# Row fetches for twenty sparse gathers on SP, and five rounds of last layers inside the last tile

## What is computed

```python
seq_embed = jnp.concatenate([emb_seq[i][seq_inputs[:, :, i]] for i in range(NB)], axis=-1)   # 2048 x 40 x 128
item_embed = jnp.concatenate([emb_seq[i][item_inputs[:, i]] for i in range(NB)], axis=-1)    # 2048 x 128
other_info = jnp.concatenate([dense_inputs] + [emb_sparse[i][sparse_inputs[:, i]] for i in range(NS)], axis=-1)
info = jnp.concatenate([q, seq_embed, q - seq_embed, q * seq_embed], axis=-1)
h = jax.nn.sigmoid(info @ att_W1 + att_b1)
h = jax.nn.sigmoid(h @ att_W2 + att_b2)
att = jax.nn.softmax(jnp.where(mask, (h @ att_Wf + att_bf)[..., 0], NEG_INF), axis=-1)
user_info = jnp.einsum('bl,bld->bd', att, seq_embed)
info_all = jnp.concatenate([user_info, item_embed, other_info], axis=-1)      # batch-normalised, then
y = sigmoid(prelu(prelu(info_all @ ffn_W1 + ffn_b1) @ ffn_W2 + ffn_b2) @ out_W + out_b)
```

## Time and profile before

| | us |
|---|---|
| median of 3 runs | 1611.01 (1609.24 to 1612.11) |
| the profiled execution | 1607.81 |
| its span | 1606.0 |
| POOL busy | 1198.4, 75% of the span, 1259 instructions |
| PE busy | 1407.4, 88% |
| DVE busy | 849.7, 53% |
| ACT busy | 398.4, 25% |
| chain that ended last | POOL 72%, issue 24%, PE 3%, DVE 1% |

### The profile page before, as it was taken

How to read it: one execution, slowest core, us unless ns; L and a number is a source line. 1 busy time by engine, 2 the same in 40 slices (tenths; PEclk the granted TensorE clock), 3 DMA queues, 4 the chain that set the end, 5 groups by cost and what they waited for, 6 DMA issues and landing times.

```text
span 1606.0 us, 25922 instructions
## 1 busy us (share of the span) xinstructions
PE 1407.4 (88%) x7602; PEld 776.3 (48%) x7602; DVE 849.7 (53%) x2102; ACT 398.4 (25%) x725; POOL 1198.4 (75%) x1259
## 2 busy tenths in 40 slices
PE   0599999998989988898988888998889998989878
PEld 0355555554545444454544455545455554545432
DVE  5744647463554646365464634646464464636453
ACT  3422213221222212121131222212222221212123
POOL 7877777777777777777777777777777777777773
PEclk9999999999999999999999999999999999999975
DMA  8411121211111121111111112121111112111121
GB/s 165 105 28 47 27 47 28 47 28 27 48 27 48 28 46 29 27 47 28 48 28 47 28 27 48 28 47 28 46 29 27 48 28 46 28 27 28 28 27 14
DMA packets 61501, 63.51 MB, mean 40 GB/s; under 512 B 35845, under 2 KB 36179, under 8 KB 61359
## 3 DMA queue, kind: packets, MB, share of 16 engines
q0 software_dynamic: 40128, 41.17, 12.6%
q1 hardware_dynamic: 19170, 12.53, 3.1%
q10 hardware_dynamic: 2062, 8.08, 1.8%
HBM read 61.57 MB, written 0.11 MB: 38 GB/s over the span
## 4 chain that ended last, share of the span: by engine, by line
POOL 72%; issue 24%; PE 3%; DVE 1%; ACT 1%; POOLq 0%; DMA 0%; DVEq 0%
POOL hist L346 70%; POOL items L346 2%; DVE sums L892 1%; PE pre L530 0%; PE pre L542 0%; PE pre L531 0%; ACT pool L632 0%; PE turned L523 0%; PE pre L442 0%; PE mid L458 0%; PE turned L524 0%; PE pre L444 0%; PE mid L451 0%; DMA hist<-in_L_rec_emb_seq_dram,idx 0%; PE sums L399 0%
## 5 line engine op out<-in xcount | busy, mean ns | idle before, releaser
L346 POOL DMA_INDIRECT hist<-in_L_rec_emb_seq_dram,idx x1184 | 1131.4, 956 | 361.0 <-issue 361.0
L412 PE MATMUL grown<-pool,split 128*128 128x384 bf16 x4704 | 849.6, 330 | 39.7 <-DVE pool L795 39.6
L412 PEld LDWEIGHTS grown<-pool,split 128*128 128x128 bf16 x4704 | 454.5, 99 | 443.9 <-issue 155.5
L795 DVE TENSOR_SCALAR pool<-rel 128x768 bf16<-128x768 bf16 x784 | 382.2, 541 | 0.0
L919 DVE TENSOR_TENSOR prod_t<-turned,item_t 128x512 f32<-128x512 f32 x160 | 109.7, 688 | 401.0 <-ACT hist_t L657 400.8
L662 ACT ACTIVATE hidden<-pre 80x512 f32<-80x512 f32 x160 | 94.9, 593 | 612.7 <-DVE pre L927 601.3
L927 DVE TENSOR_TENSOR pre<-pre,item_part 80x512 f32<-80x512 f32 x160 | 111.0, 694 | 167.5 <-PE pre L444 167.5
L425 PE MATMUL turned<-ident,hist 128*128 128x128 f32 x592 | 99.1, 288 | 86.4 <-DMA hist<-in_L_rec_emb_seq_dram,idx 85.7
L442 PE MATMUL pre<-hist_t,w_hist 128*80 128x512 f32 x320 | 164.4, 595 | 0.0
L444 PE MATMUL pre<-prod_t,w_raw 128*80 128x512 f32 x320 | 163.4, 592 | 0.0
L892 DVE SCALAR_TENSOR_TENSOR sums<-hist,weight,sums 128x128 f32<-128x128 f32 x608 | 159.8, 348 | 0.0
(11 more groups left out here) (110 smaller groups left out, 466.8 us busy)
## 6 DMA issues: line engine op xcount, KB each, us to landing
sparse_rows<-in_L_rec_emb_sparse_dram SPq DMA_DIRECT2D x1280, 0.2 KB
hist<-in_L_rec_emb_seq_dram,idx POOLq DMA_INDIRECT x1184, 2.4
keys<-key_rows SPq DMA_DIRECT2D x28, 384.0 KB
hist<-in_L_rec_emb_seq_dram ACTq DMA_DIRECT2D x6, 672.0 KB
keys<-key_rows ACTq DMA_DIRECT2D x4, 384.0 KB
hist<-in_L_rec_emb_seq_dram ACTq DMA_DIRECT2D x2, 728.0 KB
sparse_rows<-in_L_rec_emb_sparse_dram,idx_sparse POOLq DMA_INDIRECT x38, 3.3
raw<-in_r_seq_inputs_dram SPq DMA_DIRECT2D x1, 600.0 KB, 8.4
```

Of the source, the lines that this page charges most:

```text
L346: gp.indirect_dma_start(rows, None, table, bass.IndirectOffsetOnAxis(ap=index, axis=0)).then_inc(landed, 16)
L412: last = nc.tensor.matmul(grown[n][:, 0:MC], split[n][:, c, k, :], hot[:, slot, n * MC:(n + 1) * MC], start=(c == 0 and k == 0), stop=(c = ...
L795: last = nc.vector.tensor_scalar(hot[:, slot, :], rel[half][:, :, 0:RC], float(c), None, ALU.is_equal)
```

## The change

SP fetches twenty gathers in place of ten (pairs 0 to 2, and two of pair 3's six), in steps of up to six rows of one lane: all lanes for the first pair, then all lanes for the second, and so on, 512 steps in 16 stages of 32. POOL issues 28 sparse gathers: ten (the rest of pair 3, pair 4) between the gathers of tiles 14 and 15, eighteen behind tile 15. The rounds of pairs 0 to 4 stand inside the last tile, at the start of its iteration 7, on PE, ACT and DVE; their products use the PSUM banks `grown` and `sums`. The last three rounds stand where all eight did, with `USER_AT` 6.

```diff
     SHARE = 7
     ROWS_AT = ((0, 1, 2, 3, 4), (5, 6, 7, 8, 9))
     PACE = 5
-    USER_AT = 2
-    FETCHED = 10
-    LANES = P // TILES
+    USER_AT = 6
+    FETCHED = 20
+    SOONER = 5
     UP = 64
     MP = 3
     LAST = GROUPS - 1
...
-            taken = [sp.alloc_register(f"row_number{i}") for i in range(FETCHED)]
+            taken = [sp.alloc_register(f"row_number{i}") for i in range(2 * NS)]
             halves = sparse_table.rearrange("v (h e) -> v h e", h=2)
-
-            def fetch_rows(first, end):
-                for lane in range(first, end):
-                    sp.load(taken, idx_sparse[lane:lane + 1, :, :].rearrange("p t n -> p (t n)")[:, 0:FETCHED])
-                    for i in range(FETCHED):
+            lanes = [(first, lane) for first in range(0, FETCHED, 2 * NS) for lane in range(P)]
+
+            def fetch_rows(stage):
+                for first, lane in lanes[stage * len(lanes) // TILES:(stage + 1) * len(lanes) // TILES]:
+                    count = min(2 * NS, FETCHED - first)
+                    numbers = idx_sparse[lane:lane + 1, :, :].rearrange("p t n -> p (t n)")
+                    sp.load(taken[0:count], numbers[:, first:first + count])
+                    for i in range(count):
                         row = sp.snap(taken[i], min_val=0, max_val=NS * V - 1)
-                        tile, n = i // NS, i % NS
+                        tile, n = (first + i) // NS, i % NS
                         sp.dma_start(sparse_rows[lane:lane + 1, tile, n * E:(n + 1) * E].rearrange("p (h e) -> p h e", h=2),
                                      halves[bass.ds(row, 1), :, :]).then_inc(sparse_fetched[tile // 2], 16)
 
             sp.wait_ge(sparse_idx_ready, 1)
-            fetch_rows(0, LANES)
+            fetch_rows(0)
             for tile in range(TILES - 1):
                 sp.wait_ge(picked_ready, tile + 1)
                 if tile + 2 < TILES:
                     load_keys(tile % 2, tile + 2)
-                fetch_rows((tile + 1) * LANES, (tile + 2) * LANES)
+                fetch_rows(tile + 1)
...
+
+            def gather_sparse(first, end):
+                for number in range(max(first * 2 * NS, FETCHED), end * 2 * NS):
+                    tile, n = number // NS, number % NS
                     gather(sparse_rows[:, tile, n * E:(n + 1) * E], sparse_table, idx_sparse[:, tile, n:n + 1],
                            sparse_landed[tile // 2])
+
+            with gp.Fori(0, PAIRS - 1) as pair:
+                for half in range(2):
+                    gather_tile(pair * 2 + half, half)
+            gather_tile(TILES - 2, 0)
+            gp.wait_ge(sparse_idx_ready, 1)
+            gather_sparse(0, SOONER)
+            gather_tile(TILES - 1, 1)
+            gather_sparse(SOONER, PAIRS)
...
+            def ffn2(p):
+                pe.wait_ge(y1_ready, p + 1)
+                if 0 < p < SOONER:
+                    pe.wait_ge(score_ready, p)
+                to = sums if p < SOONER else mid
+                nc.tensor.matmul(to[0:H2, 0:W], fw2[:, :], y1[:, :], start=True, stop=True).then_inc(ffn2_done, 1)
+
+            def output(p):
+                pe.wait_ge(y2_ready, p + 1)
+                if p > 0:
+                    pe.wait_ge(score_ready, p)
+                to = sums[0:1, W:2 * W] if p < SOONER else pre1[1][0:1, 0:W]
+                nc.tensor.matmul(to, ow[:, :], y2[:, :], start=True, stop=True).then_inc(score_done, 1)
+
+            def sooner_rounds():
+                pe.wait_ge(part_ready, TILES - 1)
+                pe.wait_ge(picked_ready, TILES)
+                for p in range(SOONER):
+                    turn_sparse(p)
+                    if p > 0:
+                        ffn2(p - 1)
+                    ffn1(p)
+                    if p > 0:
+                        output(p - 1)
+                ffn2(SOONER - 1)
+                output(SOONER - 1)
+
                         ends = [at + 2, at + 4, at + PER]
                     else:
                         at, to, other, ends = 0, tile, half, [0, 0, 0]
+                    if last and g == SHARE:
+                        sooner_rounds()
                     if g < LAST:
                         turn_group(g + 1)
...
+            for p in range(SOONER, PAIRS):
                 turn_sparse(p)
-                if p > 0:
+                if p > SOONER:
                     ffn2(p - 1)
                 ffn1(p)
-                if p > 0:
+                if p > SOONER:
                     output(p - 1)
                 if p == USER_AT:
...
+            def sooner_rounds():
+                for p in range(SOONER):
+                    copy_sparse(p)
+                    if p > 0:
+                        add_bias2(p - 1)
+                        score_of(p - 1)
+                add_bias2(SOONER - 1)
+                score_of(SOONER - 1)
...
+            def sooner_rounds():
+                for p in range(SOONER):
+                    if p > 0:
+                        prelu2(p - 1)
+                    prelu1(p)
+                prelu2(SOONER - 1)
...
                     else:
                         first_hot, to, other = 4 + (g - SHARE - 1) * 5, tile + 1, 1 - half
                         ends = [first_hot + 3, first_hot + 5]
+                    if last and g == SHARE:
+                        pick()
+                        sooner_rounds()
                     if g < LAST:
                         product(g + 1, (g + 1) % 2)
-                    if g == SHARE:
+                    if g == SHARE and not last:
                         pick()
-                        if not last:
-                            dve.wait_ge(rel_ready, tile + 2)
+                        dve.wait_ge(rel_ready, tile + 2)
                     heat(to, other, first_hot, ends[0])
                     if g == 0:
...
```

More of the change, by code:

```diff
@@ L203, in build @@
         items_landed = [sem(f"items_landed{h}") for h in range(2)]
-        sparse_fetched = [sem(f"sparse_fetched{p}") for p in range(2)]
+        sparse_fetched = [sem(f"sparse_fetched{p}") for p in range(-(-FETCHED // (2 * NS)))]
         sparse_landed = [sem(f"sparse_landed{p}") for p in range(PAIRS)]
@@ L349, in _ @@
             gp.iota(lane[:, :], [[0, 1]], base=0, channel_multiplier=1).then_inc(lane_numbered, 1)
-            with gp.Fori(0, PAIRS) as pair:
-                for half in range(2):
-                    tile = pair * 2 + half
-                    wait(gp, idx_ready, tile + 1)
-                    wait(gp, sum_step, tile * L + PACE * G)
-                    if half == 1:
-                        wait(gp, piece_ready, PIECES)
-                    for n in range(NB):
-                        gather(items[:, half, n * E:(n + 1) * E], seq_table, idx[half][:, SEQ + n:SEQ + n + 1],
-                               items_landed[half])
-                    for g in range(GROUPS):
-                        if g == PACE:
-                            wait(gp, user_ready, tile + 1)
-                        for k in range(NB if g == LAST else G * NB):
-                            c = g * G * NB + k
-                            gather(hist[:, half, c * E:(c + 1) * E], seq_table, idx[half][:, c:c + 1],
-                                   group_landed[half][g])
@@ L369, in _, with gather_tile @@
-            gp.wait_ge(sparse_idx_ready, 1)
-            for tile in range(TILES):
-                for n in range(NS):
-                    if tile * NS + n < FETCHED:
-                        continue
+            def gather_tile(tile, half):
+                wait(gp, idx_ready, tile + 1)
+                wait(gp, sum_step, tile * L + PACE * G)
+                if half == 1:
+                    wait(gp, piece_ready, PIECES)
+                for n in range(NB):
+                    gather(items[:, half, n * E:(n + 1) * E], seq_table, idx[half][:, SEQ + n:SEQ + n + 1],
+                           items_landed[half])
+                for g in range(GROUPS):
+                    if g == PACE:
+                        wait(gp, user_ready, tile + 1)
+                    for k in range(NB if g == LAST else G * NB):
+                        c = g * G * NB + k
+                        gather(hist[:, half, c * E:(c + 1) * E], seq_table, idx[half][:, c:c + 1],
+                               group_landed[half][g])
@@ L414, in grow, with turn_sparse, ffn1 @@
                     last.then_inc(hot_used, 1)
+            def turn_sparse(p):
+                fetched = min(max(FETCHED - 2 * NS * p, 0), 2 * NS)
+                if fetched > 0:
+                    pe.wait_ge(sparse_fetched[p], 16 * P * fetched)
+                if fetched < 2 * NS:
+                    pe.wait_ge(sparse_landed[p], 16 * (2 * NS - fetched))
+                for h in range(2):
+                    rows = sparse_rows[:, 2 * p + h, :]
+                    nc.tensor.transpose(grown[0][:, h * P:(h + 1) * P], rows[:, 0:2 * E], ident[:, :])
```

(16 more changed lines are left out.)

80 lines of the change are left out of this document (27 added, 53 removed).

## The result

The changed kernel takes 1925.98 us (median of 4, 1925.28 to 1928.12) against 1611.46 before: ratio 1.1957, 95% interval 1.1936 to 1.1978. It is slower, as forecast; the forecast was 1858 us, with a range of 1752 to 1962. The profiled execution took 1926.67 with a span of 1924.9.

A forecast was written before the change was run, and what follows sets the result against it. SP's row fetches and register loads, with keys queued behind them, were taken as the bound. Last pick 1772.9 + 1.1 + 30 + 4 + 45.0 = 1853.0 span; 1854.8 profiled, plus 3.2: 1858 us, range 1752 to 1962.

The forecast's parts named there:

- SP's stage: SP's queue, first twelve stages: 32 steps take 115.0 us, 115.9 with key loads; a load of six takes 0.98.
- The term that was mis-sized: SP's register load of six numbers: 0.98 us in all of the first twelve stages, so 115.0 us a stage.
- The bounds: SP's load of six lies between 0.73 and 1.22 us, a stage between 107.1 and 122.8; 94 us to either side.
- Who waits: Keys queue behind SP's fetches; ScalarE's `relate` waits from tile 1, some 19 us there, and tiles last 115.9 us.
- From tile 12 on: From tile 12's `relate` at 1483.3 the engines run at their own pace: 289.6 us to the last pick at 1772.9.
- rival 3: GpSimd gets no lead, so the last three tiles run at 94.9 us: 25 us more, 1883; chance 0.08.
- Rival 1 and 2: SP's register load: 1, in proportion to its registers, 1764 us, chance 0.20; 2, a fixed 1.22 us, 1952, chance 0.20.
- Rival 4: SP is in time after all and only the end changes, still slower: 1620 to 1633 us; chance 0.04.
- The end: From the last pick: pick 1.1 us, rounds inside 30, low clock in groups 8 and 9 4, the rest 45.0.
- POOL: GpSimd's ten gathers ahead of the last history, 12.5 us, lie beside standing engines and cost nothing; without that cover, 12.5.

The follow-up runs named there:

- e3_keys_by_act: The changed kernel with the key loads issued by ACT in iteration 9 instead of by SP; 1823.06 us.
- e7_one_load_a_lane: The changed kernel with one register load of all twenty numbers for each lane, 128 loads and not 512; 1629.04 us.
- e5_load_sizes_used: The kernel before with eight more register loads per SP stage, of various sizes and first columns, each choosing one 8-byte fetch; span 1607.0 us.
- g1_groups_of_eight: The changed kernel with steps of 8, 8 and 4 rows, so that all loads begin on 16-byte addresses; 1666.49 us.
- e6_numbers_shifted: The changed kernel with the row numbers 8 bytes further on in SBUF, same loads of six, six, six and two; 1998.38 us.
- e8_products_keep_clock: The kernel before with spare bf16 products, whose output nothing reads, between the steps of the rounds on TensorE; 1604.46 us.

## Why the prediction was right, and where it was off

- **SP's stage.** Right in mechanism, and in size for eight of twelve stages: 116.3 measured for 115.9, the load of six 0.99 for 0.98. The middle between the bounds was taken for want of a row, and its agreement is a piece of luck: the load is neither a floor with a slope nor in proportion, but fours of aligned words.
- **The term that was mis-sized** is the load in stages 4 to 7: "a stage 115.0 us", for all twelve. The second six numbers begin 24 bytes into the tensor, off a multiple of 16, and took 1.56 us, over the upper bound of 1.22. Measured 134.4 a stage, 4 x 18.5 = 74 us; the last pick came at 1848.4 for 1772.9, 75.5 later. The bounds took it that a load's price depends on its count alone. The range held because it allowed 7.8 us to either side in all twelve stages, and only four were off, by 18.5.
- **Who waits.** As forecast: keys behind fetches, `relate` waiting from tile 1 (16.2 us, 19 forecast) to tile 12, SP's waits for picks all but gone, POOL waiting some 28 us a tile for 20 forecast. `e3_keys_by_act` shows it.
- **From tile 12 on.** `relate` at tile 12 starts at 1559.6, about 5 us behind the last late keys (issued at 1555.0); from there to the last pick 289 us, 289.6 forecast. The last three picks are 86.6, 88.3 and 85.0 us apart, not 94.9: POOL had its lead, so rival 3 did not happen.
- **Rival 1 and 2** (1764 and 1952): neither rule holds. The Trainium skill's 200 ns per register (Runtime: NRT & Kernel Launch, "Instruction fetch mechanics") is just what each word outside an aligned four takes here, 0.20 us; I had set it aside because ten registers took 1.22 and not 2.0, and ten from column 6 take 2.30. Its 600 ns floor (DMA: Bandwidth & Descriptors, "Latency and other measured facts") does not hold: one register takes 0.50 and four 0.53.
- **Rival 4** (SP in time, 1620 to 1633 us) is what `e7_one_load_a_lane` shows when the loads are few: 1629.0. The end alone makes the change slower, by 18 us against before beside it.
- **The end.** 76.5 us from the last pick, 80.1 forecast. Pick and rounds took 29.6 for 31.1: the first round ran at the full clock. From group 8 to the end 46.9, with 49.0 forecast (45.0 and 4 for the clock). With the 75.5 us of the stages these 3.6 the other way make the 71.9 between the 1853.0 forecast and the span of 1924.9.
- **POOL.** Its ten gathers ahead cost nothing with SP late, and 11.8 us with SP in time, 12.5 forecast.

## What to carry to other kernels

An engine without busy time can have a full queue: count what it issues in a period against the period, and look at what stands behind it in order; here two key loads behind 192 fetches held up everything. When work is spread over steps, a fixed price for each step grows with the count of steps: by the medians 512 loads took some 550 us where 128 took 190. And a chain of small steps moved inside other work is not hidden where every engine runs it in order: five rounds inside the last tile held group 8 for 28.5 us behind the pick, and the end did not come sooner.

## What the runs showed of the hardware

- A register load from SBUF costs, by the fit, 0.30 us, 0.225 for each four words from a 16-byte start and 0.20 for each word else (`e5_load_sizes_used`; six words 0.95 or 1.50, ten 1.18 or 2.30). `g1_groups_of_eight` and `e6_numbers_shifted` follow it, -260 and +72 us.
- A row fetch from SP costs 0.431 us of its queue, in bursts of 80 and of 192 alike.
- In before's rounds the clock did not come back: with PE busy 9.80 us of 10 by small float32 products the granted clock stays at 0.50, the 1.2 GHz level. With one spare 128x384 bf16 product behind each step, PE busy 9.77 us of 10, it stands at 1.00, the 2.4 GHz level, in the same stretch of `e8_products_keep_clock`, and a round falls from 5.30 to 3.72 us though PE does more.
